# Two-layer retention, then mixture of experts: the order of leaving and routing four sequences

## The reference

```
x = x + _L0_attn_a_ref(_layernorm(x), ...)   # two layers of retention and a feed-forward, then a layer norm (lnf)
x = x + _L0_ffn_ref(_layernorm(x), ...)      # mixture of experts, 8 experts, 2 for each token
x = x + _L0_attn_b_ref(_layernorm(x), ...)   # causal softmax attention
x = x + _L0_ffn_ref(_layernorm(x), ...)      # the same mixture again

def _L0_ffn_ref(x, gate_w, w1, w3, w2):
    probs = softmax(x @ gate_w); expert_weights, expert_indices = top_k(probs, 2)
    expert_weights = expert_weights / expert_weights.sum(-1, keepdims=True)
    for i in range(8):   # the token's weight for expert i is zero when i was not chosen
        out = out + (silu(x @ w1[i]) * (x @ w3[i])) @ w2[i] * wi[..., None]
```

## Time and profile before

| | |
|---|---|
| median of the runs | 876.16 us |
| the profiled execution | 877.76 us |
| its span, first to last instruction | 875.9 us |
| busy: TensorE matmul / DVE / ACT / POOL | 74% / 68% / 43% / 34% |
| mean granted clock of TensorE | 0.866 |
| first to last start of the first 32 scatters (L777) | 281.5 to 323.2 us |

### The profile page before, as it was taken

One profiled execution on the slowest core, in us unless ns is written; L12 is line 12 of the kernel. 1 busy time (PEld: TensorE's weight loads), 2 busy tenths in 40 slices (PEclk: granted clock), 3 DMA queues, 4 the chain that ended last, 5 costly groups with the idle time before them and its releaser, 6 DMA issues.

```text
span 875.9 us, 19341 instructions
## 1 busy us (share of the span) xinstructions
PE 651.2 (74%) x6492; PEld 450.0 (51%) x6492; DVE 593.1 (68%) x1762; ACT 372.9 (43%) x645; POOL 297.8 (34%) x602
## 2 busy tenths in 40 slices
PE   2767989999795205899925788898888971599990
PEld 1434555666363205899912244444444441599990
DVE  2684779666867833688854787677678736388874
ACT  2446557555344203344414155565464651244430
POOL 0122354454245761355513001110513132245550
PEclk9887989999897558899966598999999995699995
DMA  9300992000000216565535221322321000355544
GB/s 303 118 1 5 186 183 48 1 3 1 1 2 3 64 44 138 149 169 166 156 105 129 80 59 28 84 52 56 104 56 48 8 24 16 93 164 160 165 138 150
DMA packets 98568, 75.75 MB, mean 86 GB/s; under 512 B 8060, under 2 KB 90812, under 8 KB 98332
## 3 DMA queue, kind: packets, MB, share of 16 engines
q1 hardware_dynamic: 92872, 63.10, 29.5%
q0 software_dynamic: 4544, 9.38, 3.1%
q10 hardware_dynamic: 1056, 2.04, 0.7%
HBM read 49.32 MB, written 23.20 MB: 83 GB/s over the span
## 4 chain that ended last, share of the span: by engine, by line
PE 35%; DVE 14%; DMA 6%; issue 5%; SPq 4%; POOL 3%; ACT 2%; ACTq 0%; DVEq 0%; POOLq 0%
PE PC L2037 7%; PE PA L2027 5%; DVE rmax L1377 4%; PE PB L2027 4%; PE P L2115 4%; PE PA L2075 3%; PE PA L2073 3%; POOL rows_dram L777 3%; DMA ffn_w<-in_w 2%; PE PC L2098 1%; PE PB L2098 1%; SPq L617 1%; SPq L620 1%; DVE X L1324 1%; DMA R<-outs_dram 1%
## 5 line engine op out<-in xcount | busy, mean ns | idle before, releaser
L1377 DVE TENSOR_REDUCE rmax<-PA 128x1 f32<-128x512 f32 (+3 forms) x256 | 120.0, 488 | 49.8 <-PE PA L2075 42.9
L789 POOL DMA_INDIRECT outs_dram<-va,ids x78 | 81.1, 1040 | 107.2 <-DVE va L1316 104.1
L2037 PE MATMUL PC<-ffn_w,pm 128*128 128x128 f32 x624 | 88.4, 285 | 12.3 <-DMA ffn_w<-in_w 12.0
L2037 PEld LDWEIGHTS PC<-ffn_w,pm 128*128 128x128 f32 x624 | 76.9, 194 | 14.4 <-DMA ffn_w<-in_w 13.8
L1675 ACT ACTIVATE kv_b<-P 128x256 f16<-128x256 f16 x78 | 29.9, 384 | 127.7 <-PE P L2016 127.7
L2075 PE MATMUL PA<-kst,qst 96*128 96x512 bf16 (+3 forms) x256 | 84.0, 333 | 0.0
L2073 PE MATMUL PA<-mqb,idb 128*128 128x128 bf16 x256 | 60.4, 237 | 25.9 <-DVE rmax L1377 18.4
L1306 DVE SCALAR_TENSOR_TENSOR pm<-PB,invb,decay 128x512 f32<-128x512 f32 x78 | 58.5, 750 | 21.0 <-ACT decay L1683 12.9
L2073 PEld LDWEIGHTS PA<-mqb,idb 128*128 128x128 bf16 x256 | 25.3, 99 | 88.2 <-DVE rmax L1377 48.3
L2027 PE MATMUL PA<-kv_b,pm 128*128 128x128 f16 x936 | 67.9, 224 | 0.0
L2027 PE MATMUL PB<-kv_b,pm 128*128 128x128 f16 x936 | 67.0, 223 | 0.0
(11 more groups left out here) (254 smaller groups left out, 1492.7 us busy)
## 6 DMA issues: line engine op xcount, KB each, us to landing
ffn_w<-in_w SPq DMA_DIRECT2D x78, 256.0 KB, 3.0
rows_dram<-wall SPq DMA_DIRECT2D x1, 8385.0 KB, 52.3
proj_w<-rows_dram SPq DMA_DIRECT2D x78, 65.0 KB, 1.9
qst<-parts_dram SPq DMA_DIRECT2D x48, 96.0 KB
kst<-parts_dram SPq DMA_DIRECT2D x48, 96.0 KB
parts_dram<-qkp SPq DMA_DIRECT2D x16, 256.0 KB, 2.8
qst<-in_w SPq DMA_DIRECT2D x8, 256.0 KB, 6.0
kst<-in_w SPq DMA_DIRECT2D x8, 256.0 KB, 7.4
```

The source lines that it names most:

```text
L789: nc.gpsimd.indirect_dma_start(out=outs_dram, out_offset=bass.IndirectOffsetOnAxis(ap=ids[:, k % YB:k % YB + 1], axis=0), in_=ysb[:, k % Y ...
L1377: nc.vector.tensor_reduce(rmax[:, i, h % HG:h % HG + 1], PA[:, n % 2, 0:(i + 1) * P], AX_X, ALU.max).then_inc(pair_sb[n % 2], 1)
L2037: ins = mm(PC[:, k % 2, 0:D], eT[:, k % 2, f, :], w2b[k % WB2][:, f, :], start=f == 0, stop=f == FB - 1)
```

## The change

Sequence 0 leaves in two pieces, `leave_sums(0)` behind t = 28 and `leave_rows(0)` behind t = 29, and its factors are made by DVE behind t = 30 instead of by POOL. It is turned at t = 31, its router and `route(0, 0)` are at t = 32 inside the tile loop, and its counts directly behind the loop. The factors of unit 6 are made by POOL at t = 29 instead of t = 30. Behind retention DVE chooses sequence 0's slots first; sequences 1 and 2 leave together (`leave(1, 2)`, factors of both at once in `pair_factors`), and sequence 3 in two pieces around the routing of sequence 1. Exponentials and shares of the first mixture are made once for all sixteen tiles (`exp_all`, `all_shares`), behind the tables; ranks and differences of all sequences are kept for that. `low_rows` goes ahead of `pick_slots`, whose last instruction now releases POOL; the second mixture has this order too. POOL loses the factors of sequences 0, 1 and 2. `routing_tables` moves behind `leave_and_route`.

```diff
@@ ring_plan
         if n == UNITS:
             plan += [("router", 0, 0)]
+        if n >= 2:
+            plan += [("up", n - 2, f) for f in range(FB)]
...
-        if n == UNITS + 1:
+        if n == UNITS:
             plan += [("count", 0, 0)]
...
+        if n == UNITS - 1:
+            plan += [("turn", LNM1, 0)]
-    for s in range(1, SEQ):
-        plan += route(0, s) + [("count", 0, s)]
+    plan += route(0, 1) + [("turn", LNM1, 2), ("count", 0, 1), ("router", 0, 2), ("count", 0, 2)]
+    plan += route(0, 3) + [("count", 0, 3)]
@@ POOL
+                    if n == UNITS - 1:
+                        norm_factors(STAT[ln_up(n - 1)])
...
-                if u == 2 and n >= 1:
+                if u == 2 and 1 <= n < UNITS - 1:
                     norm_factors(STAT[ln_up(n - 1)])
...
-                if t == LAST - 1:
-                    norm_factors(STAT[(LNM1, 0)])
...
-            norm_factors(STAT[(LNM1, 1)])
             add_ffn2(UNITS - 1)
-            norm_factors(STAT[(LNM1, 2)])
@@ DVE, tile loop
+                    if t == LAST - 4:
+                        leave_sums(0)
+                    if t == LAST - 3:
+                        leave_rows(0)
+                    if t == LAST - 2:
+                        mean_factors(STAT[(LNM1, 0)])
...
+                    if t == LAST:
+                        route(0, 0)
...
-                    if t == LAST - 3:
-                        leave(0)
@@ DVE, leave_and_route
                 mean_factors(STAT[ln_up(UNITS - 1)])
-                leave(1)
-                route(0, 0)
+                choose_slots(0, 0)
                 add_ffn(UNITS - 2)
-                leave(2)
-                choose_slots(0, 0)
+                leave(1, 2)
+                pair_factors(STAT[(LNM1, 1)])
                 add_ffn(UNITS - 1)
+                leave_sums(3)
                 route(0, 1)
                 choose_slots(0, 1)
-                leave(3)
+                leave_rows(3)
                 mean_factors(STAT[(LNM1, 3)])
-                for s in (2, 3):
-                    route(0, s)
-                    choose_slots(0, s)
+                route(0, 2)
+                choose_slots(0, 2)
+                route(0, 3)
+                choose_slots(0, 3)
@@ DVE, new: shares of all sequences
+            def all_shares():
+                dve.wait_ge(lg_e, SEQ)
+                link(nc.vector.scalar_tensor_tensor(out=share, in0=flat(all_ranks), scalar=1.0, in1=flat(all_exps),
+                                                    op0=ALU.is_equal, op1=ALU.mult))
+                link(nc.vector.tensor_reduce(second, share.rearrange("p (t e) -> p t e", e=E), AX_X, ALU.add))
+                link(nc.vector.tensor_scalar(total, second, 1.0, None, ALU.add))
+                link(nc.vector.reciprocal(w12[:, :, 0], total))
+                nc.vector.tensor_tensor(w12[:, :, 1], w12[:, :, 0], second, ALU.mult)
@@ ACT, blocks, n == UNITS
+                        keep_logits(0, 0).then_inc(freed("router", 0, 0), 1)
+                        high_rows(0, 0)
...
+                        keep_counts(0, 0).then_inc(freed("count", 0, 0), 1)
@@ ACT, experts(0)
+                    normalize(LNM1, 1)
+                    logits(0, 1)
+                    normalize(LNM1, 2)
+                    plain_turn(LNM1, 2)
+                    high_rows(0, 1)
+                    keep_counts(0, 1).then_inc(freed("count", 0, 1), 1)
+                    keep_logits(0, 2).then_inc(freed("router", 0, 2), 1)
+                    high_rows(0, 2)
+                    keep_counts(0, 2).then_inc(freed("count", 0, 2), 1)
+                    normalize(LNM1, 3)
+                    logits(0, 3)
+                    high_rows(0, 3)
+                    keep_counts(0, 3).then_inc(freed("count", 0, 3), 1)
+                    exp_all()
@@ TensorE, blocks
+                    if t == LAST:
+                        router(0, 0).then_inc(ring_ps, 1)
                     if u < 2 and n >= 2:
                         up(n - 2, 2 * u, 2 * u + 2)
-                    if t == LAST:
-                        plain_turn(LNM1, 0)
-                    if t == LAST + 1:
-                        router(0, 0).then_inc(ring_ps, 1)
...
+                    if t == LAST - 1:
+                        plain_turn(LNM1, 0)
+                count(0, 0).then_inc(ring_ps, 1)
                 down(UNITS - 2)
                 plain_turn(*ln_up(UNITS - 1))
                 up(UNITS - 1, 0, FB)
-                count(0, 0).then_inc(ring_ps, 1)
                 down(UNITS - 1)
```

More of the change, by code:

```diff
@@ L367, in mixer_kernel @@
         rank = sb("rank", [P, 2, TPS, E])
+        all_ranks, all_exps = (late[:, 2 * L + i * NT * E:2 * L + (i + 1) * NT * E].rearrange(
+            "p (s k e) -> p s k e", s=SEQ, k=TPS) for i in range(2))
+        share, second, total = (scratch[0][:, o:o + n] for o, n in ((0, NT * E), (NT * E, NT), (NT * E + NT, NT)))
         taken = sb("taken", [P, 2, TPS * E], BF16)
@@ L1103, in add_ffn, with leave_sums @@
                 wait_ring(dve, "down", c)
-            def leave(s):
-                for k in range(TPS):
-                    ins = nc.vector.bn_stats(st6[:, k, :], R[:, TPS * s + k, :])
+            def leave_sums(*seqs):
+                for i, s in enumerate(seqs):
+                    for k in range(TPS):
+                        ins = nc.vector.bn_stats(st6[:, TPS * i + k, :], R[:, TPS * s + k, :])
                 link(ins)
-                for k in range(TPS):
+                for k in range(TPS * len(seqs)):
@@ new lines, in leave, with pair_factors @@
+            def leave(*seqs):
+                leave_sums(*seqs)
+                leave_rows(*seqs)
+            def pair_factors(b):
+                dve.wait_ge(stats_sb, b + 2)
+                dve.wait_ge(nrm_sb, b)
+                dve.wait_ge(xn_act, b)
+                v, y, z, w = (nrm[:, :, k, :] for k in range(4))
+                link(nc.vector.tensor_scalar(v, mvr[:, :, :, 1], EPS, None, ALU.add))
+                link(nc.vector.tensor_scalar(y.bitcast(I32), v.bitcast(I32), -0.5, float(0x5f3759df),
+                                             ALU.mult, ALU.add))
+                for _ in range(3):
+                    link(nc.vector.tensor_tensor(z, y, y, ALU.mult))
+                    link(nc.vector.scalar_tensor_tensor(out=z, in0=z, scalar=-0.5, in1=v, op0=ALU.mult,
+                                                        op1=ALU.mult))
+                    link(nc.vector.scalar_tensor_tensor(out=y, in0=z, scalar=1.5, in1=y, op0=ALU.add,
+                                                        op1=ALU.mult))
+                nc.vector.scalar_tensor_tensor(out=w, in0=y, scalar=-1.0, in1=mvr[:, :, :, 0], op0=ALU.mult,
+                                               op1=ALU.mult).then_inc(nrm_sb, 2)
@@ L1338, in experts @@
                     leave_and_route()
+                    routing_tables()
                 else:
@@ L1342, in experts @@
                 tile_tables(m)
+                if m == 0:
+                    all_shares()
                 expert_weights(0, expert_of(0))
@@ L2039, in down @@
                     ins.then_inc(m2_ps, 1)
-                for s in range(1, SEQ) if m == 0 else (SEQ - 1,):
-                    route(m, s)
-                    count(m, s).then_inc(ring_ps, 1)
+                if m == 0:
+                    route(0, 1)
+                    plain_turn(LNM1, 2)
+                    count(0, 1).then_inc(ring_ps, 1)
+                    router(0, 2).then_inc(ring_ps, 1)
+                    count(0, 2).then_inc(ring_ps, 1)
+                route(m, SEQ - 1)
+                count(m, SEQ - 1).then_inc(ring_ps, 1)
                 wait_ring(pe, "count", m, SEQ - 1)
```

103 lines of the change are left out of this document (52 added, 51 removed).

## The result

The changed kernel took 862.45 us (median of 4 executions, 860.83 to 866.60) beside 875.46 of the kernel before: ratio 0.9864, 95% interval 0.9816 to 0.9911, so 11.9 us faster (7.8 to 16.1); the medians lie 13.0 apart. Its profiled execution took 866.60 around a span of 864.8. The forecast was 869.3, range 866.3 to 873.2: the sign is right, the time lies 3.9 us under the range.

What follows compares the result with a forecast made beforehand. The bound was when POOL may begin its scatters, late because DVE is late, and whether it stays fed. Scatters ending 7.2 us earlier plus 0.3 for the port gave -6.9, off 876.16: 869.3 us, range 866.3 to 873.2.

Steps and rivals of the forecast that it cites:

- The sums fit the gap before sequence 1's logits: On DVE after retention: leave_sums(3), 3.49 us, ends at 278.1, and DVE still waits 1.5 us for logits at 279.6.
- the scatters' run: On POOL: 24 scatters kept fed from 285.7, taking 31.26 us without the surplus hole, ending at 316.96, 7.2 us earlier.
- the 0.3 for the port: Shared DVE and POOL port: 0.3 us added for the bias add and three small copies now beside other work.
- I take the difference off the median: Final step for the whole kernel: -6.9 us applied to the earlier runs' median 876.16, giving 869.3 us.
- the swap of low_rows and pick_slots moves nothing: In the second mixture-of-experts layer: the new order costs or gains nothing, the same instructions standing ahead of the semaphore.
- Half clock in tiles 30 and 31: TensorE's retention there: full clock expected; if pauses of some 2.3 us still bring half clock, 1 us comes back.
- B: Rival, 0.20: sequence 1 later than 285.4 through half clock, ring order, bias add, or sequence 2 missing POOL; 872.0 us.
- a clock near 0.5 in 235 to 240: Sign that the forecast is wrong: TensorE's granted clock near 0.5 in the window 235 to 240 us.
- the wait of 1.13 that was to go: DVE in tile 30: its 1.13 us wait for the retention vanishes, since that is done by 237.2 at full clock.
- C: Rival, 0.08: retention's DVE pauses hide more of the moved work, 1.5 to 3 us more gain; 867 us.
- D: Rival, 0.05, slower: nothing put into the retention loop is hidden, scores 31 and all after 4.8 us later; 877.2 us.
- E: Rival, 0.04: the stretch shortens but the expert phase behind the last scatter gives it back; 875 us.

Runs made afterwards that it cites:

- f1: The changed kernel again, unedited, with a further profile; ratio 0.9817 to the kernel before, median 867.63 us of 6.
- e6: Changed kernel with sequence 3's leave_sums moved behind sequence 1's slots; profile only: ninth scatter unmoved against e1, last 3.6 us later.
- e7: Changed kernel with shares of sequences 1 to 3 again made per sequence; profile only: ninth scatter 1.98 us later, last 2.64.
- e5: Changed kernel with sequences 1 and 2 leaving one by one, each with own factors; profile only: tile 28 to last scatter 99.28 us against 97.09.
- e9: Changed kernel with 46 small POOL operations ahead of the first eight scatters; profile only: tile 28 to last scatter 97.21 us against 97.09.
- e2: Changed kernel with 23 small chained POOL operations ahead of the last eight scatters; ratio 0.9972 to the kernel before, mean 872.23 us.
- e3: Changed kernel with the old order of low_rows and pick_slots in the attention (second mixture); ratio 0.9936 to the kernel before.
- f2: The same edit as e3, timed again: changed kernel with the old order in the attention; ratio 0.9927 to the kernel before.
- e1: The changed kernel again, unedited, for a second profile; ratio 0.9899 to the kernel before, median 866.83 us of 12.
- f3: The kernel before, unedited, profiled once more; no separate time given, mean of all its 91 executions 874.87 us.
- e8: Changed kernel with leave(0) whole behind tile 29; profile only: tile 28 to last scatter 102.19 us against 98.69 in the changed kernel's first profile.
- e10: Changed kernel with three orders changed: sequence 1's high rows and counts sooner, sequence 3's turn ahead of sequence 2's counts; ratio 0.991 to the kernel before.

## Why the prediction was right, and where it failed

**Right: the mechanism and nearly every position.** Where the half clock stays away from tiles 30 and 31, as the forecast had it, the positions up to the ninth scatter are good to 0.3 us. Execution f1, retention of tile 30, and its ninth scatter:

```profile
237.80 1.08 PE L2010 MATMUL PC<-pm,va 128*32 128x128 f32 x32
```

```profile
287.61 1.07 POOL L778 DMA_INDIRECT rows_dram<-qst,idx  x1 [15.26 <-DVE qst L1293]
```

Counted from keys 28: scores 29 late by 1.0 (measured 0.9: 8.29 against 7.37), keys 30 early by 2.5 (2.6: 15.28 against 17.87), down(6) at 36.1 (f1: 36.0), logits of sequence 3 at 80.9 (81.0), ninth scatter at 66.4 (66.3). The sums fit the gap before sequence 1's logits with 1.5 us over (1.75 measured, e6), the shares are off the path (e7), the pair saves time that reaches the ninth scatter (e5), the early first eight are worth nothing (e9), and the experts give nothing back (e2).

That the stretch as a whole came to 6.7 against 6.9 is in part luck. In the three profiles it ends 0.3 us later than forecast: 1.1 late at the ninth scatter by the half clock, 0.6 early by the scatters' run, and the 0.3 for the port not spent. In f1, which has the clock that the sum assumed, the stretch gained 8.0.

**The failed step is the last one**, "I take the difference off the median", with its range. It set -6.9 against three executions within 2.3 us, and made the range from doubts about the changed stretch alone. Executions of one kernel spread by 3.5 us (standard deviation), and the first four of the changed kernel had a mean 2.1 under that of all 22. A median of a few had to be given some 2 us either way on top (an estimate from the 3.5). The forecast was 6.8 us over the measured median: 1.3 since the three executions stood over the mean of 91 (876.16 against 874.87), 2.7 since the first four of the changed kernel stood under the mean of 22 (862.45 against 865.14), and 2.8 since the gain in the means is 9.7 and not 6.9. So with the whole sample 865.1 would still have lain 1.2 under the range: towards that stand two terms that the sum did not have.

**A term taken as nothing:** "the swap of low_rows and pick_slots moves nothing: the same instructions stand ahead of the semaphore". True of that semaphore, but between them stand the maxima of the next use, 0.69 us sooner: 0.70 us at the exponentials 56 to 59 and another 0.15 at 96 to 99 with the changed first half. I followed the instructions moved to their own consumer and not what stood behind the first of them.

**A term not foreseen:** half clock in the attention, 1.5 us less on average in these profiles. 6.7 + 0.85 + 1.5 = 9.05, against 9.7 (7.6 to 11.9). The last part is a difference of samples and not a shown effect of the change, and the 0.65 that remain lie within the interval.

**Sizes within the stretch.**
- Half clock in tiles 30 and 31: forecast gone, with 1 us kept as a bound (B). That step failed as well: of the eleven profiles in which sequence 0 leaves in two pieces, the retention of tile 30 took 1.08 us in one (f1) and 1.82 to 1.94 in ten, and that of tile 31 took 1.94 in three (the changed kernel's first, e3, f2). TensorE pauses 2.19 us before 233.75 in the changed kernel, and 1.70 before 240.75, and the retention takes 1.94 behind each (next fence). f1 has pauses of 2.19 and 2.08 at the same two places and the full clock. Windows 235 to 245 of the changed kernel, then 240 to 245 of e1, then 235 to 240 of f1 (width, PE, PEld, DVE, ACT, POOL, clock):

```profile
234.77 1.94 PE L2010 MATMUL PC<-pm,va 128*32 128x128 f32 x32
...
241.86 1.94 PE L2010 MATMUL PC<-pm,va 128*32 128x128 f32 x32
```

```profile
235.00:240.00 5.00, 4.05 (x44) 2.42 (x36) 3.63 (x16) 0.84 (x3) 1.04 (x3) 0.75 0.00 0
240.00:245.00 5.00, 4.25 (x44) 3.49 (x45) 3.98 (x10) 1.65 (x4) 1.99 (x3) 0.66 0.01 3
```

```profile
240.00:245.00 5.00, 4.54 (x60) 4.13 (x61) 4.02 (x9) 1.60 (x4) 2.00 (x3) 1.00 0.01 3
```

```profile
235.00:240.00 5.00, 2.93 (x44) 2.25 (x48) 4.93 (x18) 1.65 (x4) 3.70 (x12) 1.00 0.00 0
```

  From tile 28 to the ninth scatter that makes 66.3, 67.3 and 68.9 us (f1, e1, changed kernel): 0, 1.0 and 2.6 late. The bound of 1 was too small, since the second tile can be hit as well. The sign that was given, a clock near 0.5 in 235 to 240, came in part (0.75), and the wait of 1.13 that was to go is there with 1.03; only f1 has no hole over 0.5 on DVE in tiles 28 to 31.
- The scatters' run: I had 30.3 us from the ninth's start to the last one's, measured 29.7. They meet fewer of DVE's large instructions: 23.6 us of POOL for 24 scatters, 24.2 to 24.3 in four of the five profiles with the old first half (23.6 in f3). The 0.3 I added for the port was of the wrong sign.
- B's other parts did not come: sequence 2 was just in time (hole 0.40), and down(6) starts 36.0 us behind keys 28 in f1, against 37.2 before; in the changed kernel's first profile the half clock puts it at 38.6.
- C (retention hides more) did not come: up to keys 31 the changed kernel gained 0.8 to 1.9 us, forecast 1.7. That C's 867 lies nearer to 865.1 than the forecast does is chance. D and E (slower) are refuted by the stages and e2. With the half clock in both tiles on both sides, leave(0) in one piece costs 3.5 us (e8 against the changed kernel's first profile), so the split is over half of the gain by itself. The single prices, 3.5 + 2.4 + 3.6 + 2.6, exceed the 6.7 together: each was taken with the others in place. What the routing of sequence 0 inside the loop brings, and the factors moved from POOL to DVE, was not tried alone.

## What to carry to other kernels

Before a range is written, ask how far executions of the same kernel lie apart, and in which unchanged stage; three that agree say little, and a gain is read more sharply between two instructions around the change than from the totals. A stream on one engine that is fed by another has a first part whose start is worth nothing: what counts is the item behind the hole, and work belongs into the wait ahead of that item. When an order is swapped, follow what stood between the two and not only what both end in.

## What the hardware showed

- The time of an execution goes with its mean granted clock: over 87 of the kernel before (0.857 to 0.877), a straight line gives 7.0 us per 0.01 and leaves about 2 us of the 3.5. Tiles 0 to 28 alone, the same in all, took 189.0 to 199.6.
- A scatter beside a large DVE instruction can take up to 1.58 us on POOL instead of 0.96, by how the two starts meet. Beside the low rows of a sequence (0.68 us, float16 out of float32), over all 17 profiles: 1.42 us where the scatter began 0.10 us behind them (e10, once), 1.31 or 1.32 where it began 0.20 behind (nine times, all in kernels with the old first half), 0.97 at 0.55 behind, and 0.95 or 0.96 in all 23 cases in which the scatter had begun first. Beside one copy of weights (0.69 us) it was 1.29 where the scatter began 0.23 behind the copy, and 1.32 where the copy began 0.50 behind the scatter (L1297, before); the 1.58 of e10 stands beside two copies. This took back all of e10's 1 us. The Trainium skill, "SBUF — State Buffer", section "Who interferes with whom", says that a two-port copy keeps GpSimd from writing descriptors; the traces agree in kind, with 0.33 and 0.36 us of delay at one copy of 0.69. L1300, which makes the low rows, is no copy and delayed a scatter by 0.46 all the same.
